# A state-space block and an expert block on one core: softplus with a GpSimd step, a shorter norm, another order of the start, and a new timetable

## What is computed

```python
h = x * rsqrt(mean(x * x) + EPS) * norm_scale          # of the layer-normed x
xs, res = split(h @ w_in)                              # 512 + 512 channels
res = silu(res)
xs = silu(causal_depthwise_conv(xs, conv_w, conv_b))   # 4 taps
delta, B, C = split(xs @ w_xproj)                      # 16, 16, 16
delta = softplus(delta @ w_dt + b_dt)
deltaA, deltaBx = exp(delta * -exp(A_log)), (delta * xs) * B   # 16 states
ys = scan(a_i * a_j, a_j * b_i + b_j)                  # along the tokens
out = ((einsum(ys, C) + xs * D) * res) @ w_out + x
```

## Time and profile before

| what | us |
|---|---|
| median of 3 runs | 2507.78 (2499.76 to 4268.07) |
| the profiled execution | 2508.51 |
| its span, first to last instruction | 2506.7 |
| busy: TensorE | 2175.4 |
| busy: VectorE | 2185.3 |
| busy: ScalarE | 1845.7 |
| busy: GpSimd | 1857.7 |

### The profile page before, as it was taken

One profiled execution on the slowest core, in us unless ns is written; L12 is line 12 of the kernel. 1 busy time (PEld: TensorE's weight loads), 2 busy tenths in 40 slices (PEclk: granted clock), 3 DMA queues, 4 the chain that ended last, 5 costly groups with the idle time before them and its releaser, 6 DMA issues.

```text
span 2506.7 us, 35858 instructions
## 1 busy us (share of the span) xinstructions
PE 2175.4 (87%) x9268; PEld 1311.2 (52%) x9268; DVE 2185.3 (87%) x2820; ACT 1845.7 (74%) x3897; POOL 1857.7 (74%) x1324
## 2 busy tenths in 40 slices
PE   4666789899898989989898989989898998988787
PEld 2434546464554645555464646556464655646454
DVE  0389989898999989899898989999898999989931
ACT  4656686878878786887878787787868788785644
POOL 1668778787878878797877878787887878777620
PEclk9785899999998999999899999999999999999999
DMA  5111011111102011110101110110211111011100
GB/s 109 43 38 38 22 51 35 56 35 45 38 18 68 26 56 36 54 32 31 54 24 56 35 55 32 39 47 22 60 32 56 35 35 47 22 52 37 35 1 17
DMA packets 83400, 101.69 MB, mean 41 GB/s; under 512 B 23480, under 2 KB 49872, under 8 KB 83168
## 3 DMA queue, kind: packets, MB, share of 16 engines
q1 hardware_dynamic: 83168, 99.06, 13.1%
HBM read 90.13 MB, written 8.91 MB: 40 GB/s over the span
## 4 chain that ended last, share of the span: by engine, by line
PE 31%; DVE 27%; issue 19%; ACT 12%; POOL 5%; DVEq 1%; ACTq 0%; DMA 0%; POOLq 0%; SPq 0%
PE bank L758 18%; DVE h L1300 13%; DVE yT L1316 8%; PE stateT L931 7%; PE bank L906 3%; POOL bx L728 3%; ACT decay L1174 3%; ACT cum_sb L1139 2%; DVE xs L1211 2%; PE bank L892 2%; DVE yT L1313 1%; ACT rows L967 1%; DVE cumT L1255 1%; ACT scratch L1092 1%; DVE prod L1282 1%
## 5 line engine op out<-in xcount | busy, mean ns | idle before, releaser
L728 POOL TENSOR_TENSOR bx<-dx,B_rows 128x1024 f32<-128x1024 f32 x512 | 1199.9, 2363 | 229.5 <-DVE h L1300 197.6
L1300 DVE TENSOR_TENSOR_SCAN h<-decay,bx 128x512 f32<-128x512 f32 x1024 | 1240.1, 1211 | 83.3 <-ACT decay L1174 69.4
L1174 ACT ACTIVATE decay<-delta,decay_rate 128x512 f32<-128x512 f32 x1024 | 705.6, 693 | 316.7 <-DVE h L1300 315.2
L931 PE MATMUL stateT<-ident,h 128*128 128x128 f32 x4096 | 655.8, 293 | 209.0 <-DVE h L1300 126.8
L931 PEld LDWEIGHTS stateT<-ident,h 128*128 128x128 f32 x4096 | 497.6, 149 | 548.8 <-issue 294.6
L1316 DVE SCALAR_TENSOR_TENSOR yT<-stateT,C_tok,yT 128x512 f32<-128x512 f32 x960 | 698.1, 727 | 48.4 <-PE stateT L931 46.5
L758 PE MATMUL bank<-q_to_expert,xnT 128*128 128x512 f32 x512 | 264.4, 643 | 5.2 <-DVE xs L1211 5.2
L758 PE MATMUL bank<-k_to_expert,cumT 128*128 128x512 f32 x512 | 249.8, 611 | 11.6 <-DVE prod L1282 11.5
L1139 ACT ACTIVATE cum_sb<-bank,gate 128x64 f32<-128x64 f32 x1024 | 222.4, 326 | 32.7 <-PE bank L758 30.9
L758 PE MATMUL bank<-hT,w_in_sb 128*128 128x512 f32 x512 | 244.3, 607 | 1.7 <-ACT scratch L1030 0.9
L906 PE MATMUL bank<-expert_to_out,prodT 128*128 128x256 f32 x1024 | 241.3, 379 | 0.5 <-ACT cum_sb L1139 0.5
(11 more groups left out here) (168 smaller groups left out, 2615.1 us busy)
## 6 DMA issues: line engine op xcount, KB each, us to landing
B_rows<-B_scratch SPq DMA_DIRECT2D x256, 256.0 KB, 3.2
x_front<-in_L_attn_x SPq DMA_DIRECT2D x16, 512.0 KB, 5.2
x_back<-in_L_attn_x SPq DMA_DIRECT2D x16, 512.0 KB, 3.6
out<-x_back SPq DMA_DIRECT2D x16, 512.0 KB, 3.2
w_in_sb<-in_L_attn_w_in SPq DMA_DIRECT2D x1, 1024.0 KB, 5.9
h<-in_L_ffn_V_fwd SPq DMA_DIRECT2D x2, 256.0 KB
h<-in_L_ffn_W_inv_exp SPq DMA_DIRECT2D x2, 256.0 KB
h<-in_L_ffn_W_fwd SPq DMA_DIRECT2D x2, 256.0 KB
```

The lines of the kernel that those rows point to most:

```text
L728: pool.tensor_tensor(bx[use % BX_RING][:, :, :], dx[q.parity][:, 2 * half:2 * half + 2, :], row, ALU.mult).then_inc(s_bx.step(f"{n},{half} ...
L931: last = pe.transpose(stateT[j % 2][:, c * P:(c + 1) * P], h[n % 2][:, c, j * P:(j + 1) * P], ident[:, :])
L1174: act.activation(decay[c % 2][:, :], delta[q.parity][:, c, :], ACT.Exp, scale=decay_rate[:, c, n:n + 1]).then_inc(s_exp.step(f"{n},{c}"), 1)
L1300: dve.tensor_tensor_scan(h[n % 2][:, c, :], decay[c % 2][:, :], bx[(2 * n + c // 2) % BX_RING][:, c % 2, :], 0.0, ALU.mult, ALU.add).then_ ...
```

## The change

- Softplus: the passes v and u on ScalarE are gone. GpSimd's `w_task` starts with a new operation s: v = (e + 1) - 1 in one two-step instruction from e, waits for it, and forms w as before. It waits for ex (not u) and for d1 of the chunk that had its place of scratch before.
- The front's norm: ScalarE's sums now give -mean, its squares (x - mean)^2 without the factor D. GpSimd does five operations: two additions, two pow, one multiplication. The factor of both norms comes from one pow; the constants left over go into the norm weights (one small ScalarE copy, once) and into `keep`.
- The head: the weights that the front needs have a semaphore of their own, `front_ld`, are loaded first, and are waited for only where they are used (`xs_task` on TensorE, `hT_task` on ScalarE). The decay rates' exp and VectorE's constants stand at beat 24 of period -1. The 22 jobs stand in period 0, beside batch 0's scan, from beat 1, in the four banks of the front's tasks, at beats that a small planner picks: at least 3 apart, in a bank that no task of the front uses from 8 beats after a fill of it (14 ahead of its own fill) on, with ScalarE's copy 6 beats behind TensorE. The raw weights lie in tiles of the back stages (`rows`, `x_back`, `cum_sb`, `prod`, `xnT`, `cumT`, `prodT`, `o_rows`, `gate`). The scan no longer waits for the jobs; the first tasks of the back stages do, and SP's load of `x_back` of batch 0, which moves to slot 15.
- `scan_part` on GpSimd waits for dx1 ahead of the period's first bx and for dx3 ahead of the second (before: dx3 ahead of the first).
- Some 60 of the table's beats are others.

```diff
-JOBS_FROM, JOBS_EVERY = 60, 3
+JOBS_FROM, JOBS_EVERY = 1, 3
+KEPT_AFTER = 6
+READ_WITHIN = 14
+LATE = 24
-    ("B", "keep", "pool"): (255,),
+    ("B", "keep", "pool"): (260,),
...
-    ("F", "sq", "act"): (11,),
-    ("F", "rs", "pool"): (19,),
+    ("F", "sq", "act"): (13,),
+    ("F", "rs", "pool"): (16,),
     ("F", "h", "act"): (16,),
-    ("F", "hT", "pe"): (18, 25),
-    ("F", "hT", "act"): (22, 29),
-    ("F", "x", "sp"): (93,),
-    ("F", "xs", "pe"): (32, 34, 36, 38),
-    ("F", "xs", "act"): (34, 36, 38, 43),
+    ("F", "hT", "pe"): (17, 19),
+    ("F", "hT", "act"): (24, 31),
+    ("F", "x", "sp"): (72,),
+    ("F", "xs", "pe"): (31, 34, 36, 38),
+    ("F", "xs", "act"): (34, 36, 38, 39),
...
-    ("F", "silu", "act"): (71,),
+    ("F", "silu", "act"): (70,),
...
-    ("F", "dt", "pe"): (82, 83, 100, 107),
-    ("F", "dt", "act"): (89, 89, 106, 112),
-    ("F", "ex", "act"): (91, 97, 109, 119),
-    ("F", "ln", "act"): (93, 97, 111, 120),
-    ("F", "w", "pool"): (101, 103, 117, 126),
-    ("F", "w2", "pool"): (101, 109, 125, 126),
-    ("F", "d1", "dve"): (96, 105, 120, 123),
+    ("F", "dt", "pe"): (82, 83, 106, 107),
+    ("F", "dt", "act"): (89, 91, 106, 117),
+    ("F", "ex", "act"): (89, 95, 107, 117),
+    ("F", "ln", "act"): (93, 97, 110, 122),
+    ("F", "w", "pool"): (100, 102, 118, 123),
+    ("F", "w2", "pool"): (101, 104, 123, 126),
+    ("F", "d1", "dve"): (96, 105, 123, 123),
...
-    ("B", "logit", "act"): (342,),
-    ("B", "logit_rows", "pe"): (347,),
-    ("B", "lb", "dve"): (345,),
-    ("B", "mx", "dve"): (345,),
-    ("B", "sub", "pool"): (355,),
-    ("B", "ex", "act"): (348,),
+    ("B", "logit", "act"): (343,),
+    ("B", "logit_rows", "pe"): (343,),
+    ("B", "lb", "dve"): (343,),
+    ("B", "mx", "dve"): (344,),
+    ("B", "sub", "pool"): (352,),
+    ("B", "ex", "act"): (347,),
...
-    ("F", "dx", "pool"): (103, 111, 126, 127),
-    ("L", "x", "pool"): (479, 480),
-    ("L", "store", "sp"): (477,),
+    ("F", "dx", "pool"): (108, 111, 126, 128),
+    ("L", "x", "pool"): (476, 480),
+    ("L", "store", "sp"): (462,),
...
                 pool.sem_inc(passed["pool"], 1)
-                r = r_x0[b.parity]
-                rstd(f_pool, b, None, var_f[:, :], 2.0 ** -24, None, ve_f, r, None, ("ve", "r1"))
...
+                pool.tensor_scalar(ve_f[:, :], sq_f[:, :], D * EPS, None, ALU.add).then_inc(f_pool.step("ve"), 1)
+                pool.tensor_scalar(ms_f[:, :], sq_f[:, :], D * EPS * EPS / (1 + EPS), None, ALU.add).then_inc(f_pool.step("me"), 1)
+                pool.wait_ge(f_pool.sem, f_pool.done(b, "me"))
                 pool.sem_inc(passed["pool"], 1)
...
+                pool.tensor_tensor(rs_f[:, :], ms_f[:, :], minus_half[:, :], ALU.pow).then_inc(f_pool.step("rs"), 1)
+                pool.tensor_tensor(r_x0[b.parity][:, :], ve_f[:, :], minus_half[:, :], ALU.pow).then_inc(f_pool.step("r1"), 1)
+                pool.wait_ge(f_pool.sem, f_pool.done(b, "rs"))
+                pool.tensor_tensor(nm_f[:, :], mean_f[:, :], rs_f[:, :], ALU.mult).then_inc(f_pool.step("nm"), 1)
...
                 e, v = scratch[:, c % 2, :], scratch[:, 2 + c % 2, :]
-                pool.wait_ge(f_act.sem, f_act.done(b, f"u{c}"))
+                pool.wait_ge(f_act.sem, f_act.done(b, f"ex{c}"))
+                free = b if c >= 2 else b.shift(-1)
+                if free.exists:
+                    pool.wait_ge(f_dve.sem, f_dve.done(free, f"d1{(c - 2) % 4}"))
+                pool.sem_inc(passed["pool"], 1)
+                pool.tensor_scalar(v, e, 1.0, -1.0, ALU.add, ALU.add).then_inc(f_pool.step(f"s{c}"), 1)
+                pool.wait_ge(f_pool.sem, f_pool.done(b, f"s{c}"))
                 pool.tensor_tensor(v, e, v, ALU.subtract).then_inc(f_pool.step(f"w{c}"), 1)
...
-                if n == 0 and half == 0:
-                    pool.wait_ge(f_pool.sem, f_pool.done(q, "dx3"))
+                if n == 0:
+                    pool.wait_ge(f_pool.sem, f_pool.done(q, f"dx{2 * half + 1}"))
...
-                act.activation(v, e, ACT.Identity, bias=one[:, 0:1]).then_inc(f_act.step(f"v{c}"), 1)
...
-                act.activation(v, v, ACT.Identity, bias=minus_one[:, 0:1]).then_inc(f_act.step(f"u{c}"), 1)
...
             def scan_part(q, n, beat):
-                if q.turn is None and q.const == -1 and 8 * n + beat in job_beats:
-                    keep_combined(job_beats.index(8 * n + beat))
+                if q.turn is None and q.const == -1 and 8 * n + beat == LATE:
+                    rates()
```

More of the change, by code:

```diff
@@ L371, in bank_of, with done, walk @@
             return (uses_a_period * ((batch.const + 1 + periods) % 2) + use) % 4
-        def walk(engine, name, prologue, tasks, scan_part):
+        class JobSteps:
+            sem = w_act
+            @staticmethod
+            def done(batch, i):
+                return i + 1
+        def walk(engine, name, prologue, tasks, scan_part, job_part=None):
             beats = plan(name)
@@ L395, in period @@
                     scan_part(q, at // 8, at % 8)
+                    beat = at if name == "pe" else at - KEPT_AFTER
+                    if job_part and q.turn is None and q.const == 0 and beat in job_beats:
+                        i = job_beats.index(beat)
+                        place = job_banks[i]
+                        before = held[place]
+                        job_part(i, Use(bank[place], before[0].sem, before[0].done(before[1], before[2])) if before else Use(bank[place], w_pool, 2))
+                        if name == "pe":
+                            held[place] = (JobSteps, q, i)
                     for periods, stage, task, k in beats[at]:
@@ L554, in load_x_back @@
             def load_x_back(batch):
+                if batch.turn is None and batch.const < 2:
+                    sp.wait_ge(w_act, len(jobs))
                 if batch.turn is not None or batch.const >= 2:
@@ L568, in scan_part @@
                         row_of_B(q, slot + BB_RING - 1)
-                    if slot == 12:
+                    if slot == (NS - 1 if q.turn is None and q.const == 0 else 12):
                         load_x_back(q)
@@ L666, in keep_task @@
                 pool.sem_inc(passed["pool"], 1)
[L667 removed]
+                pool.tensor_scalar(r_keep[:, :], r_x0[b.parity][:, :], D ** 0.5, None, ALU.mult).then_inc(b_pool.step("keep"), 1)
             def o_task(b, c, use):
@@ L772, in xs_task @@
             def xs_task(b, c, use):
+                if b.turn is None and b.const == 0 and c == 0:
+                    pe.wait_ge(front_ld, 16 * N_FRONT[0])
                 if c == 0:
@@ L836, in rt_task @@
                 br, m = k // 2, k % 2
+                if k == 0 and b.turn is None and b.const == 0:
+                    pe.wait_ge(w_act, len(jobs))
                 if k == 0:
@@ L911, in scan_part @@
             def scan_part(q, slot, beat):
-                if q.turn is None and q.const == -1 and 8 * slot + beat in job_beats:
-                    combine_weights(job_beats.index(8 * slot + beat))
                 if beat % 2:
@@ L920, in scan_part @@
                     return
-                if j == 0 and n == 0 and batch.turn is None and batch.const == 0:
-                    pe.wait_ge(w_act, len(jobs))
                 if j == 0:
@@ L1228, in r_task @@
                 if j == 0:
+                    if b.turn is None and b.const == 0:
+                        dve.wait_ge(w_act, len(jobs))
                     dve.wait_ge(xb_in[b.parity], b.half_count(16, 16))
@@ L1285, in scan_part @@
                 k = beat // 2
+                if q.turn is None and q.const == -1 and 8 * slot + beat == LATE:
+                    constants()
                 if beat % 2 == 0:
@@ L1290, in scan_part @@
                     n, c = slot, k
-                    if q.turn is None and q.const == 0 and n == 0 and c == 0:
-                        dve.wait_ge(w_act, len(jobs))
                     dve.wait_ge(s_exp.sem, s_exp.done(q, f"{n},{c}"))
```

194 lines of the change are left out of this document (99 added, 95 removed), and 8 rows, old and new, of the table TIMETABLE.

## The result

| what | before | after |
|---|---|---|
| median, us (4 runs each) | 2505.9 | 2547.1 |
| span of the profiled execution, us | 2506.7 | 2542.2 |
| first scan starts, us | 101.73 | 73.58 |
| steady period, us (from one write of B to DRAM to the next) | 145.03 | 148.98 |

The ratio is 1.0172, with a 95% interval of 1.0149 to 1.0196; one of the four runs before took 4268.07 us and is left out of it, so it is 2547.1 against 2504.01, the median of the other three. The forecast of 2468 us was for faster, and its range ended at 2500. The head won 28 us, and the steady part gave back 3.95 us in each period: -28.2 to the first scan, +59.5 from there to the last write of B, +4.2 behind it make the 35.5 between the two spans.

The account below looks back on a forecast made before the run. The prediction took VectorE to bound the kernel, so only its idle time could be won. From 2508.5 us it took -32 (head), +5 (jobs in period 0) and -13.5 (later periods): 2468 us, range 2425 to 2500.

Parts of the forecast that it names:

- The head: Start of the run to the first scan: small loads no longer hold ScalarE, first scan at 68.6 us, -32 us.
- The jobs in period 0: Weight jobs beside batch 0's scan load TensorE, mainly at beats 47 to 73: +5 us, from -3 to +25.
- s at 0.60 us: Softplus on GpSimd: each new one-input, two-step 128x512 operation takes 0.60 us, plus 0.08 for the wait before w.
- Is there room?: GpSimd's softplus stretch in a later period: four s add 2.7, net +1.0 us, which fits into 1.23 of slack.
- SiLU, GELU ... no gain: Later periods: SiLU, GELU and logit keep their beats or neighbours, so their VectorE waits bring no gain.
- Contention at 0.3 us each time: GpSimd beside VectorE's d1 in softplus: s can meet a d1, at 0.3 us each time, using up the slack.
- `bx` waits at loop turns: Start of every second period: the wait costs some 0.6 us instead of 1.7, 1.0 won six times.
- The `decay` wait behind `dt_task`: VectorE's 0.62 us wait in each later period: dt1 now stands behind ex0, 0.5 won, 15 times.
- that GpSimd takes the wait's place: Rival, softplus: s at 1.38 makes VectorE wait 2.9 us a period at d1_3, 2514 in all; chance 0.10.
- The jobs' rival: Period 0: jobs beside the scan bind TensorE, +25 us and not +5, 2488 in all; chance 0.18.
- the half head's: Rival, start of the run: the front waits for something other than small loads, half, 16 us, 2484; chance 0.10.
- the new beats': Rival listed second, later periods: half of GELU, logit and SiLU waits vanish, 15 x 2.8 = 42, 2426; chance 0.22.

Follow-up runs that it names:

- e5: e2 with the softplus rows of the table (w, w2, d1, dx, ex, ln, dt matmuls) as in the kernel before: 2469.60 us, ratio 0.9868 to the kernel before.
- e1: Kernel before with priced GpSimd operations added in its prologue, plus two pairs with VectorE: one addition 1.51 us, add-add 1.93, multiply-add 0.62, two-input subtraction 1.26.
- e2: Changed kernel with softplus passes v and u back on ScalarE and no s on GpSimd, new table kept: 2534.74 us, ratio 1.0145 to the kernel before.
- e10: e2 with only the table rows w and w2 as in the kernel before: 2472.77 us, ratio 0.9888 to the kernel before.
- e7: Changed kernel with s made of two multiply-adds by 1 in place of one add-add: 2517.58 us, ratio 1.0061 to the kernel before.
- e9: Kernel before with more priced GpSimd operations and four GpSimd-VectorE pairs added ahead of the work: one multiplication 1.50 us, multiply-multiply and add-multiply 0.62.

## Why the prediction was wrong

- **The head** (forecast -32, measured -28): right but for the price of s. hT was ready at 17.16 (said: 17.5), the `w_xproj` matmuls started at 38.47 (38.3), the copy behind them ended at 44.4 (45.1). The first scan came at 73.58, not 68.6. The first s started 1.35 sooner than said (47.65), but GpSimd's chain from there to the end of the first `bx` took 25.8 us and not 19.6; four s dearer by 1.33 us are 5.3 of these 6.2. Without s, with v and u on ScalarE, the first scan came at 70.54 (e5).
- **The jobs in period 0** (forecast +5): from the first scan to the write of B of batch 2 e5 took 216.4 us and the kernel before 215.95. The jobs cost nothing that shows: beside the nine at beats 47 to 73 VectorE waits 0.5 us for `stateT` in e5, where 5 were said, new waits of 2.1 stand beside the first ones, and the wait of 4.09 of the earlier trace rows has shrunk to 0.80 and 0.55. TensorE's granted clock was 0.96 in e5 from 100 to 145 us, and 0.84 before in 130 to 175, much the same stretch behind the first scan.
- **s at 0.60 us**: wrong, and the step that failed first: 1.93 alone (e1), 2.03 in the kernel. I bounded it by 0.20 below and by the two-input rows, 1.27 and 1.38 above, and took "one input" as a reason for less; it lay above the bound. The Trainium skill, GPSIMD Engine Reference, section 3.1, has one or two steps on one input at 1.03 cycles an element; by it I had 0.64, an estimate. The multiply-add agrees (0.62), the single step (1.50) and add-add (1.93) don't, and the measurement decides.
- **"Is there room?"**: wrong in two ways. I read the slack of one d1, the last (1.23), and took it for that of the stretch; d1_0 had 0.73, and four s of 2.0 must fit ahead of four d1. And I added four s and compared them with one wait, as if the time could be moved within the stretch.
- **"SiLU, GELU ... no gain" and the table's other rows at nothing**: wrong for w and w2, which I had costed inside that sum of GpSimd's time and never laid beside VectorE's order. Their two rows cost 64 us without s (e2 against e10, by ratio 0.0257 of 2499).
- **Contention at 0.3 us each time**: the mechanism was named, its size was not: 2.05 where the other operation is a `bx` and starts first. The Trainium skill, SBUF — State Buffer, section "Who interferes with whom", says that a VectorE operation with two SBUF inputs and a GpSimd one that reads SBUF shut each other out; the traces agree (2.73 in place of 0.68). I had taken from my own row the price for GpSimd when VectorE is first (1.60 for 1.27), which is the short operation's length; the other way round it is the long one's. The d1 beside that very row, which the prediction does not name, was already held by the w3 ahead of it (1.01 in place of 0.68); timeline of VectorE in the kernel before:

```profile
1091.02 1.01 DVE L1218 TENSOR_TENSOR delta<-delta,scratch 128x512 f32<-128x512 f32 x1
```

- **`bx` waits at loop turns** (forecast -6): the waits are gone altogether (8.9 us in the earlier trace rows, none listed in e5 or in the changed kernel), but `stateT` waits rose from 29.1 to 34.5 in e5. **The `decay` wait behind `dt_task`** (forecast -7.5): 42.7 us in e5, as before. A steady period of e5 takes 144.64 us, 0.4 less than before, where 0.9 was forecast.
- **The rivals**: that GpSimd takes the wait's place was the one that came true, from a price above 0.65 on. It gave 2514: with s at 2.03 its own formula, (4 x (2.03 + 0.08) - 1.42 - 0.27 - 1.23) x 15 + 4 x 1.43, would have given 88 us on top of 2468, 2556, near the 2547 measured; near by chance in part, since the table's share was not in it. I gave it 0.10 because s has one input. The jobs' rival, the half head's and the new beats' did not happen.
- **Two slips in the sums**, which do not move the forecast (the second rival would be 3 us lower): the three waits of the earlier trace rows make 8.1 us a period, not 8.3, and the GELU, logit and SiLU waits as read there are 1.80 + 2.32 + 1.9 = 6.0, not 5.65.

## What to carry to other kernels

Before an operation goes to an engine, run that very form (engine, steps, ALU operations, size) once by itself: two steps with a multiplication and two additions differ by three times here. Where the engine that bounds the kernel takes what another has just made, look at which instruction the maker issues next: if it is long and touches the same memory, it starts first (0.16 us here) and the consumer pays its whole length. And when two edits spend the same slack, try all four combinations: here each edit alone cost what both together did, and only leaving out both showed that the rest of the change was worth 1.3%.

## What the runs showed of the hardware

- GpSimd, 128x512 fp32, one input, constants 1 or -1: 0.62 us for multiply-add, add-multiply and multiply-multiply, 1.50 for one addition, subtraction or multiplication, 1.93 for add-add (3.3 ns for each further element), against 1.26 for two inputs (e1, e9). In the kernel, means of 64: add-add 2.03, multiply-add 0.72 and 0.63 (e7).
- VectorE and GpSimd in SBUF at once: whoever starts first runs at its own pace (a `bx` 2.35, multiply-add 0.62, VectorE's two-input operation 0.69), and the other is held. VectorE's ended 0.29 to 0.55 us behind GpSimd's (e9, the first three pairs); GpSimd's add-add lost 0.49 beside VectorE's 0.69 (e1).
- A VectorE operation with one input is held too where input and output lie in SBUF: an add-add of 128x512 took 2.14 in place of 0.43 (e9), a multiplication of 128x64 1.26 (16.97 in e1, behind a GpSimd operation of 16.75 to 18.18) in place of 0.20 (16.39 in e9), an addition of 128x4 1.00 in place of 0.17, beside a memset (e9).
- Where one of two inputs lies in PSUM it was not held, beside a `bx` that had started ahead of it: the scan kept its 1.21 (1096.30 and 1095.79 in the changed kernel), the product of `bank` and `cum_sb` its 0.68 (1068.16 and 1067.13).
